# A new step table for the projections, normalisations and gating inside each attention batch

## The reference

```python
# B=8 batches, N=512 tokens, D=256, M=1024 context rows, 8 heads of 64; 8 experts, top 2, FF=1024
q = layernorm(x) @ Wq;  k = ctx @ Wk;  v = ctx @ Wv            # per batch, split into heads
attn = softmax(q @ k^T * 64**-0.5);  o = attn @ v
x = x + tanh(g_xattn) * (o @ Wo + bo)
h = layernorm(x)
probs = softmax(h @ router^T);  top 2, normalised, with a capacity per expert
expert_out = (pre * silu(gate)) @ W2    # pre, gate = rows @ W1, rows @ Wg
x = x + tanh(g_ffn) * combine(expert_out)
```

## Time and profile before

| | us |
|---|---|
| median of 3 runs | 1835.0 (1834.96 to 1838.59) |
| profiled execution, device time | 1836.31 |
| its span, first to last instruction | 1834.6 |
| PE busy | 1693.5 (92%) |
| DVE busy | 1271.5 (69%) |
| ACT busy | 1056.2 (58%) |
| POOL busy | 679.0 (37%) |
| mean granted clock of TensorE | 0.979 |

### The profile page before, as it was taken

The page is one execution under the profiler, slowest core; times in us unless marked ns, Lnnn a source line. Parts: engine busy times, 40 slices in busy tenths (PEclk is TensorE's granted clock), DMA queues, the critical chain, the costliest instruction groups (busy, mean ns, idle before and its releaser), DMA issues. The chain is left out here.

```text
span 1834.6 us, 38501 instructions
## 1 busy us (share of the span) xinstructions
PE 1693.5 (92%) x13198; PEld 1538.1 (84%) x13199; DVE 1271.5 (69%) x2667; ACT 1056.2 (58%) x2229; POOL 679.0 (37%) x619
## 2 busy tenths in 40 slices
PE   5799999999999999999999997399999999999997
PEld 3688887887887887887888886299999999999997
DVE  4687887887888888887888876564554646546443
ACT  3667666666676676666676765154554545545443
POOL 3244345345345345345335333323233332333322
PEclk9899999999999999999999999599999999999999
DMA  6100001001001001001001011513323243231211
GB/s 188 36 1 24 14 22 49 15 22 48 13 24 48 13 24 48 13 24 48 13 24 36 20 40 60 180 24 104 93 35 98 29 104 92 33 99 29 33 26 28
DMA packets 65148, 85.89 MB, mean 47 GB/s; under 512 B 7208, under 2 KB 53800, under 8 KB 65008
## 3 DMA queue, kind: packets, MB, share of 16 engines
q1 hardware_dynamic: 47680, 64.08, 11.0%
q0 software_dynamic: 15984, 18.82, 5.9%
q10 hardware_dynamic: 1344, 1.20, 0.2%
HBM read 54.59 MB, written 29.48 MB: 46 GB/s over the span
## 5 line engine op out<-in xcount | busy, mean ns | idle before, releaser
L700 POOL TENSOR_SCALAR probs<-probs,row_rec 128x1024 f32<-128x1024 f32 x256 | 285.3, 1127 | 546.6 <-DVE row_rec L1526 530.2
L1065 ACT ACTIVATE pt_h<-turned 128x512 fp32r<-128x512 f32 x512 | 280.6, 601 | 244.2 <-PE turned L840 243.3
L1241 DVE TENSOR_TENSOR pt_l<-turned,pt_h 128x512 fp32r<-128x512 f32 x512 | 331.7, 681 | 19.0 <-ACT pt_h L1065 17.9
L1457 DVE TENSOR_REDUCE neg_max<-scores 128x1 f32<-128x1024 f32 x256 | 301.4, 1219 | 45.9 <-PE scores L828 45.0
L840 PEld LDWEIGHTS turned<-ident,probs 128*128 128x128 f32 x2048 | 226.4, 142 | 112.6 <-issue 49.9
L840 PE MATMUL turned<-ident,probs 128*128 128x128 f32 x2048 | 287.2, 281 | 36.0 <-DVE pt_l L1241 30.9
L1114 ACT ACTIVATE probs<-scores,neg_max 128x1024 f32<-128x1024 f32 x256 | 285.8, 1117 | 15.6 <-DVE neg_max L1457 15.4
L944 PE MATMUL ring<-pt_h,v_hl 128*128 128x256 f32 x1024 | 262.7, 294 | 7.9 <-DVE k_l L1241 5.3
L1693 DVE TENSOR_TENSOR act_f<-ffn,silu 128x256 f32<-128x256 f32 x288 | 122.2, 424 | 195.3 <-ACT silu L1195 181.9
L944 PE MATMUL ring<-pt_l,v_hl 128*128 128x256 f32 x1024 | 251.8, 283 | 0.0
L1195 ACT ACTIVATE silu<-ffn 128x256 f32<-128x256 f32 x288 | 110.7, 384 | 222.5 <-PE ffn L805 213.6
(11 more groups left out here) (221 smaller groups left out, 4064.7 us busy)
## 6 DMA issues: line engine op xcount, KB each, us to landing
w_raw<-w_t SPq DMA_DIRECT2D x16, 1024.0 KB, 5.7
e_rows<-lists SPq DMA_DIRECT2D x37, 260.0 KB, 2.7
ctx_raw<-ctx_t SPq DMA_DIRECT2D x16, 512.0 KB, 4.0
wg_raw<-wg_t SPq DMA_DIRECT2D x8, 1024.0 KB
lists<-rows SPq DMA_DIRECT2D x8, 520.0 KB, 7.9
x_in<-x SPq DMA_DIRECT2D x8, 512.0 KB, 4.9
x_sum<-x SPq DMA_DIRECT2D x8, 512.0 KB, 3.4
out<-x_sum SPq DMA_DIRECT2D x8, 512.0 KB, 3.0
```

Of the source, the lines that this page charges most:

```text
L700: nc.gpsimd.tensor_scalar(probs[:, k, :], probs[:, k, :], row_rec[:, k:k + 1], 1.0, ALU.mult, ALU.mult).then_inc(scaled, 1)
L1065: return nc.scalar.activation(dst, src, ACT.Copy)
L1241: return nc.vector.tensor_tensor(dst, src, hi_part.bitcast(F32), ALU.subtract)
L1457: nc.vector.tensor_reduce(neg_max[:, k:k + 1], scores[:, n % 2, :].rearrange("p (a c) -> p a c", a=2), AX.XY, ALU.max, negate=True).then_i ...
```

## The change

The table is replaced, and with it the places where its companions stand: the normalisation pieces of the previous batch come one step earlier (steps 6 to 10 instead of 7 to 11), POOL's `power(1)` at 8 and `normalise(1)` at 11, the bias at 14, `split_ctx` at 22 and 24 (were 24 and 26), and the second weight split of START at 23 (was 26). `NEXT_FROM` is 22. The set of jobs is the same, and so is every instruction.

```diff
 JOBS = {
-    0: [("v", 0, 3), ("w", 1, 0)],
-    1: [("w", 1, 1)],
-    2: [("k", 1, 0)],
-    3: [("v", 1, 0)],
-    4: [("k", 1, 1), ("q", 1, 0)],
-    5: [("w", 1, 2)],
-    7: [("w", 1, 3)],
-    8: [("v", 1, 1)],
-    9: [("v", 1, 2)],
-    10: [("k", 2, 0)],
-    11: [("k", 2, 1)],
-    12: [("v", 1, 3), ("q", 2, 0)],
-    14: [("h", 0, 0), ("h", 1, 0)],
-    16: [("w", 0, 0), ("w", 0, 1)],
-    18: [("q", 3, 0)],
+    0: [("w", 1, 0), ("k", 1, 0)],
+    2: [("w", 1, 1)],
+    3: [("k", 1, 1)],
+    4: [("w", 1, 2), ("q", 1, 0)],
+    6: [("w", 1, 3)],
+    7: [("v", 1, 0)],
+    8: [("v", 1, 1), ("k", 2, 0)],
+    10: [("k", 2, 1)],
+    12: [("h", 0, 0), ("v", 1, 2)],
+    13: [("q", 2, 0)],
+    14: [("v", 1, 3)],
+    15: [("q", 3, 0)],
+    16: [("h", 1, 0), ("w", 0, 0)],
+    18: [("w", 0, 1)],
     19: [("l", 0, 0)],
     20: [("k", 3, 0), ("w", 0, 2)],
-    22: [("k", 3, 1)],
-    23: [("x", 0, 0), ("x", 1, 0)],
-    24: [("w", 0, 3), ("q", 0, 0)],
-    26: [("v", 0, 0)],
-    27: [("r", 0, 0)],
-    28: [("k", 0, 0), ("k", 0, 1)],
-    29: [("v", 0, 1)],
-    31: [("v", 0, 2)],
+    21: [("k", 3, 1)],
+    22: [("x", 0, 0), ("x", 1, 0)],
+    23: [("v", 0, 0)],
+    24: [("w", 0, 3), ("k", 0, 0)],
+    27: [("q", 0, 0), ("r", 0, 0)],
+    28: [("k", 0, 1), ("v", 0, 1)],
+    29: [("v", 0, 2)],
+    30: [("v", 0, 3)],
 }
-NEXT_FROM = 23
+NEXT_FROM = 22
...
-                        if u == 9:
+                        if u == 8:
                             power(1, b - 1)
-                        if u == 12:
+                        if u == 11:
...
                             normalise(1, b - 1, x_sum, rows)
...
-                    if body.own and u == 15:
+                    if body.own and u == 14:
...
-                        if u == 24:
+                        if u == 22:
                             if body.own:
...
                             split_ctx(b + 1, 0)
-                        if u == 26:
+                        if u == 24:
                             split_ctx(b + 1, 1)
...
-                    if body is START and u in (19, 26):
+                    if body is START and u in (19, 23):
...
-                    n = {(7, 4): 0, (8, 4): 1, (9, 0): 2, (9, 3): 3, (10, 4): 4, (11, 0): 5, (11, 2): 6, (11, 4): 7}.get((u, gap))
+                    n = {(6, 4): 0, (7, 4): 1, (8, 0): 2, (8, 3): 3, (9, 4): 4, (10, 0): 5, (10, 2): 6, (10, 4): 7}.get((u, gap))
```

## The result

The new table makes the kernel 0.6% faster: median 1823.45 us (1821.27 to 1828.99, 6 runs) against 1835.56 (1832.44 to 1838.59, 6 runs) of before on the same chip. The ratio is 0.994, 95% interval 0.9921 to 0.9958. The forecast was 1809. So the sign and the range held, but of the 27 us forecast only 12 came. The profiled execution took 1822.84 us, its span is 1821.1, and this is 13.5 less than the span of before.

The account below looks back on a forecast made before the run. TensorE was taken as the bound, with gaps, and DVE as next. Six MIDDLE batches 19.2, START 3.1, FIRST 2.0 and LAST 3.0 sum to 27.3 us, off 1836.3: 1809 us, range 1796 to 1836.

Parts of the forecast that it names:

- START: Before the first scores: earlier weight splits let the first `v` start at about 18.5; 3.1 us won, bounds 0 and 6.
- the pair rule: MIDDLE, even-odd step pairs: first odd job starts at the later of work and 5.71 us plus DVE's lateness; 4.0 less a batch.
- the blocks: Six blocks of steps in a MIDDLE batch, forecast at 39.3, 16.4, 16.0, 17.25, 35.4 and 9.15 us, sum 133.5.
- the shade: MIDDLE: the 4.0 us a batch was cut by 0.8 to 3.2, for overlaps that can't be seen in a new table.
- The second `x` in step 22: Step 22: it waits for DVE to drain the bank of `o`, ending at 7.0 us instead of 5.4; pair 9.4.
- the turn of the loop "which stays": Steps 30 and 31: PE spends 2.30 us on the loop's turn, unchanged by the table; block 9.15 us against 9.68.
- the low clock of the earlier trace: First 6.4 us of batch 3 at mean clock 0.74, costing 1.7 us; two such places either way are 3.4 us.
- the port: Rival, steps 22 and 24: POOL's context splits hold DVE's gating pieces, 3.46 us late twice a batch; 1852 us, chance 0.10.
- Its own sign: The prediction is wrong if steps 0 to 9 don't shrink by 3 us or blocks behind step 22 grow over 2.
- the rival "more": Whole kernel: no shading of the MIDDLE gain and START at its full 6 us, giving 1798 us; chance 0.10.
- FIRST and LAST: First and last batch: 2.0 us won in FIRST (bounds -1 and 4), 3.0 in LAST (bounds 1 and 5).

Follow-up runs that it names:

- the best version: The changed kernel with MIDDLE written out, and in LAST alone no gating piece in the last two gaps of step 23: 1797.47 us, ratio 0.9796.

## Why the prediction was wrong

**Right: the pair rule and the blocks.** The rule (the first odd job starts at the later of "work" and 5.71 plus DVE's lateness) gave 4.0 us a batch, shaded to 3.2, and 3.24 is there where no loop disturbs it. Block by block the unrolled new table has 39.84, 16.23, 15.99, 17.51, 35.57 and 6.82 against the forecast 39.3, 16.4, 16.0, 17.25, 35.4 and 6.85 (9.15 less the turn). Unshaded, the rule was 0.8 too good, most of it in steps 0 to 9; that the shade was just 0.8 is luck, as nothing had worked it out. Of the sixteen pairs none misses by more than 0.3 us. The second `x` in step 22 waits as said: steps 22 and 23 take 9.3 us, 9.4 forecast.

**Right: START.** The first `v` was put at 18.5 us; there it is:

```profile
18.48 0.55 PE L802 MATMUL ring<-wv_h,ctx_h 128*128 128x256 f32 x1 [4.72 <-DVE xt_l L1240]
```

2.7 us were won with the loop and 3.5 unrolled, 3.1 forecast.

**The step that failed: the turn of the loop "which stays".** I took the 2.30 us of the earlier trace rows as a constant and the low clock of the earlier trace rows as chance to either side. The loop's price isn't a constant: against the same kernel unrolled, before pays 11.5 us for it and after 24.6, by the medians. In MIDDLE it is 13.8 and 23.3; of the 9.5 between them 4.9 stand at the turns and in steps 0 to 9 behind them, where the forecast had nothing. A single turn looks much the same in both; this is the one into batch 4 of after, 0.28 longer than in the earlier trace rows:

```profile
578.48 0.50 PE L827 MATMUL scores<-k_h,q_h 64*128 64x512 f32 x2 [2.58 <-issue]
```

The difference lies in how many turns are followed by the low clock (four instead of two in these executions) and in the idle time (13.1 us instead of 10.7, the longest 3.5 instead of 2.3). The idle time doesn't tell which turn the low clock follows: in after it follows one of 2.19 us and not this one of 2.58. So to call it chance was right for a single turn; that it cancels between the two tables was the error.

**The second step that failed: the port, priced but set aside.** The rival named the pair of instructions and the hold. I set it aside with an argument on the first split alone: it would begin 0.8 us after step 22 and be done at 4.3, when the first piece comes at 4.0. That was sound: it begins 0.36 after the step and ends at 3.9, and the piece comes at 3.94. For the second split, in step 24, I gave no argument, and there the pieces are caught. POOL begins it 0.3 us before PE begins step 24, straight behind the scaling, when DVE is at the pieces of step 23. It costs 2 us in two of six batches, 4.1 in all, not two holds in each; in the forecast it stood at nothing.

**Its own sign.** The prediction called itself wrong if the first block didn't shrink by 3. With the loop it went from 42.98 to 40.28 in batch 4, 2.7 less, so the sign came; unrolled it is 3.2 less. And one sum of it doesn't come out: the rival "more" adds to 6 x 4.0 + 6 + 2.0 + 3.0 = 35.0, which gives 1801 and not 1798. It changes nothing above.

**FIRST and LAST.** I took 2.0 and 3.0; they gave -0.1 and 0.45, and unrolled 0.7 and 0.9. Neither was worked out step by step as MIDDLE was, and "the first block wins as in MIDDLE" was the only argument for LAST. It does win there (43.01 to 40.42), but 0.7 goes in steps 22 to 29 (33.73 to 34.45) and 1.7 in 14 to 21, where moved work stands. In FIRST steps 0 to 13 win 2.6 us and steps 14 to 29 lose 3.2, where a MIDDLE batch loses 1.1 (unrolled): my -1 to 4 held it, the value taken didn't. FIRST also varies by itself: the kernels with the new table took 137.8 to 139.5 for it.

So 13.8 us are missing: MIDDLE 9.2 (about half at and behind the turns, half by held pieces), LAST 2.5, FIRST 2.1, START 0.4, less 0.5 won in the rest.

**Left open.** Why the loop costs the new table more, and how often the low clock follows a turn of either table, which would need traces of several executions. Whether PE's idle time at the turn is the loading of instructions. What decides the start of DVE against POOL: in batch 1 DVE loses with no turn ahead of it. Taking five kernels with the same pieces there (after, its unrolled version, two batches in a turn, `v 0 3` in step 31, and the best version), none of 25 batches with DVE 0.02 us or more ahead has a held piece, and of five with the two within 0.01 us three have. No kernel was run in which POOL's split waits for the gate piece.

## What to carry to other kernels

Read a hardware loop's turn as a stage of its own, over all passes: its idle time, the clock behind it and the steps that it upsets; compare the passes with each other before taking one of them for all, and the mean clock of several executions before counting low stretches in one. Where a schedule is to be judged, unroll the loop in both versions first: that shows what the schedule is worth and what the loop takes. And before moving a long GpSimd instruction, list VectorE's instructions with two SBUF inputs near every one of its new places, down to hundredths of a microsecond; if the margin is less than the scatter between passes, price the hold into the forecast and don't leave it to a rival.

## What was unexpected of the hardware

The turn of a hardware loop over a long body left TensorE idle for 2.1 us in before and 2.6 in after (10.7 and 13.1 in five turns, up to 3.5), and with what follows it, the held pieces left out, it cost 2.8 and 3.8 us a turn; unrolling alone made the old kernel 11.5 us and the new one 24.6 us faster. Behind such a turn the granted clock was 0.74 over 6.44 us in two of five cases, in four of five, and with one job moved by a step in five of five (0.52 in two of these), each count from one execution. No batch of MIDDLE of an unrolled kernel had it. Transfers of instructions stand close around each turn.

A VectorE operation of 0.18 us with two SBUF inputs took 1.08 or 1.09 when it began level with a GpSimd instruction of 1.05, in three of five such cases, 1.95 to 2.28 when it began 0.1 to 0.5 us behind one of 2.38, and 0.18 when it began 0.02 us or more ahead.
